# Transposes and scores share one ring of seven PSUM banks, and the exponentials run in forward order

## The chip, the cores and the metric

The kernel runs on the 8 cores of one Trainium2 chip, one batch element on each core, with no exchange between them. The metric is the device time in microseconds (us) of the slowest core. An engine name in the profile stands for: PE the matrix engine's matmuls, PEld its weight loads, DVE the vector engine, ACT the scalar engine, POOL the GpSimd engine. Each engine runs its own queue in order, and waits on semaphores that the others raise. PSUM, where PE writes its results, has 8 banks of 128 x 512 fp32.

## The reference

For each of 8 batch elements x is 2048 positions x 2048 features in fp32. There are 16 query heads of 128 features, and one key and one value head that all of them share:

```
q = (x @ q_w.T + q_b)  as 16 heads of 128;  k = x @ k_w.T + k_b;  v = x @ v_w.T + v_b
scores = q @ k.T / sqrt(128), masked causally
attn = softmax(scores);  out = (attn @ v, heads joined) @ o_w.T + o_b
x = layernorm(x + out)
x = layernorm(x + x @ (ffn_weight * scale_weight[:, None]).T + ffn_bias)
```

## The kernel before

All matmuls are in bf16. Everything is kept transposed, features on the partitions. The program is written as one list of operations in order; each engine takes its own from the list in that order, so the order of the list is the order of every queue. An operation names the events that it waits for.

*Stage A* computes k, v and the 16 heads of q into `KT`, `Vsb` and `QTO` (L259).

*Attention.* The outer loop runs over c = 0 to 3, four chunks of 512 queries. With c, the keys that count grow: 512 (c + 1). In it `step` runs over the heads, and `j` over the four blocks of 128 queries of the chunk. One head and one j are called a unit here; there are 64 units in each c. Three things are written into the list for each j, each for another head, so that they can overlap:

```
if 1 <= step <= H:          tr_unit(step - 1, c, j)
if step >= 2 and j <= c:    av_unit(step - 2, c, j)
if step < H:                sc_soft(step, c, j, sc_mms(step, c, j))
```

- `sc_mms` (L344, L353): PE computes the scores of a unit in c + 1 chunks of up to 512 keys, one bank each. The last chunk is 128 (j + 1) wide, and a second matmul adds the causal mask to it.
- `sc_soft`: DVE takes the maximum of each chunk (L372, into `mpart`), then the negative maximum over them (L376, `negm`). ACT takes the exponential of each chunk into SBUF and sums each as it goes (L393, `expS`). DVE adds the sums (L405, `den`; with one chunk that is left out) and takes the reciprocal (L410, `rcp`). ACT scales a 128 x 128 identity by it (L414, `diagP`). The exponentials go over the chunks in reversed order.
- `tr_unit` (L436): PE multiplies every 128 x 128 block of the exponentials with `diagP`, which transposes and normalizes it. Four blocks are a group and fill a bank; a unit has c + 1 groups. Each group is copied to SBUF as bf16 (`expST`), by DVE (L458) and by ACT (L462) in turn.
- `av_unit` (L480): PE multiplies four 128-key blocks of V with the transposed probabilities of a whole head, into the bank `psO`. The first of a head waits for all its transposed copies; after the last, ACT copies `psO` to SBUF (L489).

Steps 16 and 17 of each c have transposes and V matmuls alone.

*The PSUM banks.* The scores have a ring of five, the four banks of `psS` and `psU`; a chunk takes the next one, and waits until the exponential of what was in it is done. The transposes have two, `psT0` and `psT1`, in turn, given out by `use_bank`, which waits for the copy of what was in it. The eighth is `psO`.

*The last stage* does the output projection (L760), the two layer norms and the feed-forward (L826), in blocks of 512 positions. It gives `psT0`, `psT1`, `psU` and `psO` out by `use_bank`, and its matmuls wait for the end of the attention. Its weights come from HBM.

Of the kernel before, what the change touches and what calls it, by code (L numbers as in the profile page):

```python
# [16 lines left out]
S = 2048  # L17
H = 16
DK = 128
NT = 16  # L20
NCH = 4
W = 512
# [55 lines left out]
def build_program(serial=False):  # L78
# [25 lines left out]
    p = Prog(serial=serial)  # L104
# [4 lines left out]
    with st:  # L109
# [18 lines left out]
        psS = ps("psS", [128, 2048], F32)  # L128
        psT0 = ps("psT0", [128, W], F32)
        psT1 = ps("psT1", [128, W], F32)  # L130
        psO = ps("psO", [128, W], F32)
        psU = ps("psU", [128, W], F32)
# [5 lines left out]
        bank_evac = {"psT0": None, "psT1": None, "psO": None, "psU": None}  # L138
        rot_idx = [0]

        def use_bank(mm_emit, evac_emit):
            b = rot_idx[0] % len(pool_banks)
            rot_idx[0] += 1
            key, bk = pool_banks[b]
            mmw = [bank_evac[key]] if bank_evac[key] else []
            e_mm = mm_emit(bk, mmw)
            e_ev = evac_emit(bk, [e_mm])
            bank_evac[key] = e_ev
            return e_mm, e_ev

        with nc.sbuf_tensor("QTO", [128, NT * S], BF16) as QTO:
# [17 lines left out]
            with stA:  # L169
# [56 lines left out]
                for g in range(4):  # L226
# [16 lines left out]
                    _, E_vsb = use_bank(mmVT, evVT)  # L243
# [4 lines left out]
                for ot in range(NT):  # L248
# [4 lines left out]
                        waits=wq, inc="qw%d" % (ot % 2))  # L253
                    for c in range(NCH):
# [23 lines left out]
                        e_mm, e_ev = use_bank(mmQ, evQ)  # L278
# [5 lines left out]
            for q in range(4):  # L284
# [12 lines left out]
            expS8 = stB2.enter_context(  # L297
                nc.sbuf_tensor("expS8", [128, 8 * S], BF16))
            expST2 = stB2.enter_context(
                nc.sbuf_tensor("expST2", [128, 2 * NT * W], BF16))  # L300
            diagP = stB2.enter_context(
                nc.sbuf_tensor("diagP", [128, 8 * 128], BF16))
# [6 lines left out]
            E_trib = p.op("sync", lambda e: e.dma_start(  # L309
                out=trib_s[:], in_=tri_h), waits=[E_Q_all], inc="cst")  # L310

            ring_ap = [psS[:, s * W:(s + 1) * W] for s in range(4)] + [psU]
            ring_ev = [None] * 5
            ring_i = [0]

            E_comb2 = [[None] * 4, [None] * 4]
# [2 lines left out]
            E_exall2 = [[[] for _ in range(4)], [[] for _ in range(4)]]  # L319
            E_diag2v = [[None] * 4, [None] * 4]  # L320
            E_trmm2 = [[None] * 4, [None] * 4]
            E_trevV = [None, None]
            E_trevA = [None, None]
            E_trevall = [[], []]
            E_msd = [None, None]
            oev = [None]
            trctr = [0]

            def sc_mms(h, c, j):
                par = h % 2  # L330
                qt = 4 * c + j
                kext = (qt + 1) * 128
                nkc = (kext + W - 1) // W
                chunks = []
                for kc in range(nkc):
                    wdt = min(W, kext - kc * W)
                    s = ring_i[0] % 5
                    ring_i[0] += 1
                    slot = ring_ap[s]
                    w0 = [ring_ev[s], E_qevac[h][c], E_kevac[NCH - 1],  # L340
                          E_Q_all]
                    diag_chunk = (kc == nkc - 1)
                    p.op("tensor", lambda e, slot=slot, h=h, qt=qt, kc=kc,
                         wdt=wdt, dgc=diag_chunk: e.matmul(  # L344
                        slot[:, 0:wdt],
                        QTO[:, h * S + qt * 128: h * S + qt * 128 + 128],
                        KT[:, kc * W: kc * W + wdt],
                        start=True, stop=(not dgc), skip_group_check=True),
                        waits=w0,
                        inc=(None if diag_chunk else "t"))  # L350
                    if diag_chunk:
                        E_mm = p.op("tensor", lambda e, slot=slot, wdt=wdt:
                                    e.matmul(  # L353
                            slot[:, wdt - 128:wdt], ident_s[:], trib_s[:],
                            start=False, stop=True, skip_group_check=True),
                            waits=[E_trib], inc="t")
                    else:
                        E_mm = ("t", p.counts["t"])
                    chunks.append((s, slot, wdt, kc, E_mm))
                return chunks  # L360

            def sc_soft(h, c, j, chunks):
                par = h % 2
                qt = 4 * c + j
# [5 lines left out]
                for s, slot, wdt, kc, E_mm in chunks:  # L370
# [3 lines left out]
                        waits=[E_mm, E_comb2[par][j]], inc="v"))  # L374
# [4 lines left out]
                    waits=mx_all + E_exall2[par][j], inc="v")  # L379
                E_ex = None  # L380
                ex_all = []
                for s, slot, wdt, kc, E_mm in reversed(chunks):
                    if nkc == 1:
                        acc = den8[:, ncol:ncol + 1]
                        wx = [E_comb2[par][j], E_trmm2[par][j],
                              E_diag2v[par][j]]
                    else:
                        acc = dpart[:, mcol + kc:mcol + kc + 1]
                        wx = [E_comb2[par][j], E_trmm2[par][j],
                              E_dsum2[par][j]]  # L390
                    E_ex = p.op("scalar", lambda e, slot=slot, wdt=wdt,
                                kc=kc, ncol=ncol, acc=acc, par=par, qt=qt:
                                e.activation(  # L393
                        expS8[:, (par * 4 + qt % 4) * S + kc * W:
                              (par * 4 + qt % 4) * S + kc * W + wdt],
                        slot[:, 0:wdt], AF.Exp,
                        bias=negm8[:, ncol:ncol + 1], scale=1.0,
                        accum_out=acc), waits=wx, inc="a")
                    ring_ev[s] = E_ex
                    ex_all.append(E_ex)  # L400
# [19 lines left out]
            def tr_unit(h, c, j):  # L420
                par = h % 2
                qt = 4 * c + j
                base = par * NT * W
                if j == 0:
                    E_trevall[par] = []
                last_mm = None
                for g in range(c + 1):
                    cnt = min(4, qt + 1 - 4 * g)

                    def mmTR(bk, w, g=g, cnt=cnt, par=par, qt=qt, j=j):  # L430
                        w = w + [E_diag2v[par][j]] + E_exall2[par][j]
                        for i in range(cnt):
                            kt = 4 * g + i
                            ev = p.op("tensor",
                                      lambda e, bk=bk, i=i, kt=kt, par=par,
                                      qt=qt: e.matmul(  # L436
                                bk[:, i * 128:(i + 1) * 128],
                                expS8[:, (par * 4 + qt % 4) * S + kt * 128:
                                      (par * 4 + qt % 4) * S +
                                      (kt + 1) * 128],  # L440
                                diagP[:, (par * 4 + qt % 4) * 128:
                                      (par * 4 + qt % 4 + 1) * 128],
                                start=True, stop=True),
                                waits=(w if i == 0 else ()),
                                inc=("t" if i == cnt - 1 else None))
                        return ev

                    def evTR(bk, w, g=g, cnt=cnt, j=j, base=base):
                        dst = expST2[:, base:base + NT * W].rearrange(
                            "p (t w) -> p t w", t=NT)[  # L450
                            :, 4 * g:4 * g + cnt, j * 128:(j + 1) * 128]
                        srcv = bk[:, 0:cnt * 128].rearrange(
                            "p (t w) -> p t w", t=cnt)
                        eng = "vector" if trctr[0] % 2 == 0 else "scalar"
                        trctr[0] += 1
                        if eng == "vector":
                            ev = p.op("vector", lambda e, d=dst, s=srcv:
                                      e.tensor_copy(d, s), waits=w, inc="v")  # L458
                            E_trevV[par] = ev
                        else:  # L460
                            ev = p.op("scalar", lambda e, d=dst, s=srcv:
                                      e.copy(d, s), waits=w, inc="a")  # L462
                            E_trevA[par] = ev
                        E_trevall[par].append(ev)
                        return ev
                    e_mm, _ = use_bank(mmTR, evTR)
                    last_mm = e_mm
                E_trmm2[par][j] = last_mm

            def av_unit(h, c, pj):  # L470
# [22 lines left out]
            for c in range(NCH):  # L493
                for sl in range(2):
                    ev = None
# [37 lines left out]
            with stC:  # L533
# [15 lines left out]
                pool_banks[:] = [("psT0", psT0), ("psT1", psT1),  # L549
                                 ("psU", psU), ("psO", psO)]  # L550
                bank_evac["psO"] = E_attn_done

                OROT, OD = 5, 4
                FROT, FD = 3, 2
# [459 lines left out]
```

How the kernel before makes its waits and increments, by code:

```python
    def emit(self, eng_name, eng, sems):  # L62
        hi = {}
        for idx, (name, fn, waits, inc) in enumerate(self.ops):
            if name != eng_name:
                continue
            for s, v in waits:
                if hi.get(s, 0) < v:
                    eng.wait_ge(sems[s], v)
                    hi[s] = v
            ins = fn(eng)
            if inc is not None:
                if ins is None:
                    ins = eng.nop()
                ins.then_inc(sems[inc], SEMS[inc])
# [2 lines left out]
def build_program(serial=False):  # L78
# [863 lines left out]
                        pend[k]()  # L942
                    if pend_end is not None:
                        pend_end()
                    if bi + 1 < len(blocks):
                        preload(*blocks[bi + 1])
                    pend, pend_end = make_tail(kind, c)
                for k in range(len(pend)):
                    pend[k]()
                p.op("gpsimd",
                     lambda e: e.wait_ge(sems["od"], 16 * NT * NCH))
        nc._prog = p
        with nc.Block() as block:
```

## Time and profile before

| | us |
|---|---|
| median of 3 runs | 2586.69 (2586.14 to 2586.77) |
| the profiled execution, its own time | 2588.11 |
| its span on the slowest core, core 0 | 2586.6 |
| spans of the other cores | 2579.0 to 2584.9 |
| PE / DVE / ACT busy on core 0 | 1553.8 / 925.2 / 918.5 |
| mean granted clock of PE, core 0 | 0.753 |

The profile is of one execution, on its slowest core. Busy time is a mean over stages that differ: stage A ends at about 355 us, the attention runs to 1851 us, the last stage from there. A row of the timeline has the start and the duration in us, the engine, the line, the operation, what it writes and reads, how many instructions are merged in it, and in brackets for how long the engine stood before it and what it waited for. In the windows, a number behind x in parentheses counts instructions, and the clock is the share of full speed that was granted to PE.

### The profile page before, as it was taken

What the parts mean: (1) busy time and instruction counts of PE and PEld (TensorE: products, weight loads), DVE (VectorE), ACT (ScalarE), POOL (GpSimd) and SP (SyncE); (2) the same over time, 40 slices, a digit from 0 to 9 for tenths busy, and PEclk for the clock granted to TensorE, in tenths of its full rate; (3) what the DMA queues carried; (4) which work ended last, traced back from release to release, by engine and by line L of the source; (5) the groups of instructions that cost most, each with busy time, mean ns of one, the idle gap of its engine ahead of it and who ended that gap; (6) DMA issues with size and microseconds to landing.
All of it is one profiled execution on the core that took longest, in us unless ns stands there. A gap on an engine that the chain in (4) does not pass through costs nothing.

```text
span 2586.6 us, 25298 instructions; the slowest of 8 cores (2579.0 to 2586.6 us)
## 1 busy us (share of the span) xinstructions
PE 1553.8 (60%) x7077; PEld 723.6 (28%) x7216; DVE 925.2 (36%) x1985; ACT 918.5 (36%) x2270; POOL 374.6 (14%) x399
## 2 busy tenths in 40 slices
PE   0999925455544444444344445444798968968874
PEld 0444412222222222222222222222333323323321
DVE  0000024455543333433444444444216640632444
ACT  0211126555554444444444444444312321411411
POOL 0000100000000000000000000000266526535432
PEclk9999955566665666666666666666899979979976
DMA  9112698000000000000000000000255344344352
GB/s 156 24 33 41 82 111 110 1 1 1 1 1 1 1 1 0 1 1 1 1 1 1 1 1 1 1 0 1 66 171 155 107 151 149 126 163 127 101 136 98
DMA packets 43638, 137.03 MB, mean 53 GB/s; under 512 B 5835, under 2 KB 5868, under 8 KB 42988
## 3 DMA queue, kind: packets, MB, share of 16 engines
q1 hardware_dynamic: 28988, 84.02, 10.7%
q0 software_dynamic: 5296, 34.60, 9.9%
q10 hardware_dynamic: 9216, 16.78, 2.0%
q8 instruction: 61, 1.00, 0.2%
q14 instruction: 77, 0.63, 0.1%
HBM read 153.21 MB, written 33.55 MB: 72 GB/s over the span
## 4 chain that ended last, share of the span: by engine, by line
PE 43%; ACT 19%; DVE 16%; issue 12%; DMA 5%; another core or an unknown queue 2%; POOL 1%; DVEq 1%; ACTq 0%; SPq 0%; POOLq 0%
ACT expS L393 15%; PE psT L259 9%; PE psO L480 8%; DVE mpart L372 8%; PE psT L826 4%; PE psT L436 4%; PE psS L344 3%; PE psT L760 3%; DVE expST L458 3%; PE psU L826 2%; DMA wost<-wo_bf 2%; PE psU L760 2%; PE psO L826 2%; DMA trib_s<-tri 1%
## 5 line engine op out<-in xcount | busy, mean ns | idle before, releaser
L436 PE MATMUL psT<-diagP,expS 128*128 128x128 bf16 x2176 | 270.1, 284 | 687.3 <-DVE expST L458 536.8
L372 DVE TENSOR_REDUCE mpart<-psS 128x1 f32<-128x512 f32 (+3 forms) x512 | 289.9, 603 | 538.5 <-PE psS L353 366.5
L393 ACT ACTIVATE expS<-psS,negm 128x512 bf16<-128x512 f32 (+3 forms) x512 | 314.3, 620 | 448.2 <-DVE negm L376 447.2
L436 PEld LDWEIGHTS psT<-diagP,expS 128*128 128x128 bf16 x2176 | 200.4, 128 | 767.0 <-issue 762.4
L787 POOL TENSOR_TENSOR ycs<-yscr,xres 128x512 f32<-128x512 f32 x64 | 82.4, 1288 | 1674.5 <-ACT yscr L776 1562.8
L480 PE MATMUL psO<-expST,Vsb 128*128 128x512 bf16 x602 | 271.9, 599 | 48.7 <-ACT expST L462 41.7
L458 DVE CAST expST<-psT 128x512 bf16<-128x512 f32 (+1 forms) x320 | 204.1, 638 | 87.3 <-PE psT L436 86.4
L344 PE MATMUL psS<-KT,QTO 128*128 128x512 bf16 (+3 forms) x486 | 216.5, 531 | 26.6 <-ACT expS L393 22.2
L259 PE MATMUL psT<-xTbf,qwst 128*128 128x512 bf16 x1003 | 220.1, 379 | 1.3 <-ACT Vsb L241 0.2
L462 ACT CAST expST<-psT 128x512 bf16<-128x512 f32 (+3 forms) x320 | 155.8, 487 | 80.9 <-PE psT L436 80.9
L405 DVE TENSOR_REDUCE den<-dpart 128x1 f32<-128x2 f32 (+2 forms) x192 | 29.9, 156 | 414.2 <-ACT expS L393 414.2
L414 ACT ACTIVATE diagP<-ident_s,rcp 128x128 bf16<-128x128 bf16 x256 | 102.7, 401 | 144.2 <-DVE rcp L410 144.2
L760 PE MATMUL psT<-QTO,wost 128*128 128x512 bf16 x500 | 125.6, 406 | 24.2 <-DMA wost<-wo_bf 22.3
L826 PE MATMUL psT<-x1T,fwst 128*128 128x512 bf16 x500 | 123.5, 401 | 23.9 <-DMA fwst<-fw_bf 11.7
L259 PEld LDWEIGHTS psT<-xTbf,qwst 128*128 128x128 bf16 x1024 | 100.1, 98 | 121.0 <-issue 0.4
L625 DVE TENSOR_SCALAR rowb<-psS 1x512 f32<-1x512 f32 x8 | 5.4, 681 | 321.1 <-PE psS L605 321.1
L480 PEld LDWEIGHTS psO<-expST,Vsb 128*128 128x128 bf16 x640 | 81.6, 139 | 129.6 <-issue 123.6
L393 ACT ACTIVATE expS<-psU,negm 128x512 bf16<-128x512 f32 (+3 forms) x128 | 79.4, 621 | 103.7 <-DVE negm L376 103.2
L850 POOL TENSOR_TENSOR ycs<-zscr,ycs 128x512 f32<-128x512 f32 x64 | 88.6, 1384 | 170.4 <-ACT zscr L842 170.4
L273 ACT ACTIVATE QTO<-psT,qbs_s 128x512 bf16<-128x512 f32 x64 | 44.0, 687 | 177.5 <-PE psT L259 172.0
L344 PEld LDWEIGHTS psS<-KT,QTO 128*128 128x128 bf16 x512 | 71.3, 142 | 125.5 <-issue 123.0
L393 ACT ACTIVATION_READ_ACCUMULATOR expS<-psS,negm 128x1 f32 x512 | 102.1, 199 | 0.0
(76 smaller groups left out, 1727.8 us busy)
## 6 DMA issues: line engine op xcount, KB each, us to landing
wost<-wo_bf SPq DMA_DIRECT2D x64, 512.0 KB, 4.4
fwst<-fw_bf SPq DMA_DIRECT2D x64, 512.0 KB, 3.8
xres<-xT ACTq DMA_DIRECT2D x64, 256.0 KB, 4.6
outT<-ycs SPq DMA_DIRECT2D x64, 256.0 KB, 3.2
xTbf<-xT POOLq DMA_DIRECT2D x1, 8192.0 KB, 56.9
qwst<-qw POOLq DMA_DIRECT2D x16, 512.0 KB, 5.1
wo_bf<-wo POOLq DMA_DIRECT2D x4, 2048.0 KB, 77.3
fw_bf<-fw POOLq DMA_DIRECT2D x4, 2048.0 KB, 95.7
```

What stands on the lines that cost most here:

```text
L259: e.matmul(bk[:], qwst[:, (ot % 2) * D + dt * 128: (ot % 2) * D + dt * 128 + 128], xTbf[:, dt * S + c * W: dt * S + c * W + W], start=(dt ...
L344: wdt=wdt, dgc=diag_chunk: e.matmul(slot[:, 0:wdt], QTO[:, h * S + qt * 128: h * S + qt * 128 + 128], KT[:, kc * W: kc * W + wdt], start=T ...
L372: mc=mcol + kc: e.reduce_max(mpart[:, mc:mc + 1], slot[:, 0:wdt], axis=AX.X),
L393: e.activation(expS8[:, (par * 4 + qt % 4) * S + kc * W: (par * 4 + qt % 4) * S + kc * W + wdt], slot[:, 0:wdt], AF.Exp, bias=negm8[:, nco ...
L414: ncol=ncol: e.activation(diagP[:, (par * 4 + j) * 128:(par * 4 + j + 1) * 128], ident_s[:], AF.Identity, bias=0.0, scale=rcp8[:, ncol:nco ...
L436: qt=qt: e.matmul(bk[:, i * 128:(i + 1) * 128], expS8[:, (par * 4 + qt % 4) * S + kt * 128: (par * 4 + qt % 4) * S + (kt + 1) * 128], diag ...
L458: e.tensor_copy(d, s), waits=w, inc="v")
L462: e.copy(d, s), waits=w, inc="a")
L480: base=base: e.matmul(psO[:], Vsb[:, kt * 128:(kt + 1) * 128], expST2[:, base + kt * W: base + (kt + 1) * W], start=(kt == 0), stop=(kt == ...
L760: ot=ot: e.matmul(bk[:], wost[:, (ot % 2) * D + ht * 128: (ot % 2) * D + ht * 128 + 128], QTO[:, ht * S + c * W: ht * S + c * W + W], star ...
L826: ot=ot: e.matmul(bk[:], fwst[:, (ot % 2) * D + dt * 128: (ot % 2) * D + dt * 128 + 128], x1T[:, dt * W:(dt + 1) * W], start=(dt == 0), st ...
L850: pbuf=pbuf: e.tensor_tensor(pbuf[:, ot * W:(ot + 1) * W], zscr[:, (ot % 3) * W:(ot % 3) * W + W], pbuf[:, ot * W:(ot + 1) * W], AluOpType ...
```

## The change

The transposes leave `use_bank`. Scores and transposes take their banks from one ring of seven in the order in which PE does them: `psS` (four), `psU`, `psT0`, `psT1`. The wait for a slot is the copy or the exponential that read it last. The work of each operation stays. The exponentials of a unit go over its chunks in forward order. Ahead of the last stage `psT0`, `psT1` and `psU` are marked as free from the end of the attention on. The lambdas of the transposing matmuls and of the copies are the same as before, but for `skip_group_check=True`, and are left out here.

```diff
-            ring_ap = [psS[:, s * W:(s + 1) * W] for s in range(4)] + [psU]
-            ring_ev = [None] * 5
+            ring_ap = ([psS[:, s * W:(s + 1) * W] for s in range(4)]
+                       + [psU, psT0, psT1])
+            ring_ev = [None, None, None, None, None,
+                       bank_evac["psT0"], bank_evac["psT1"]]
             ring_i = [0]
...
-                    s = ring_i[0] % 5
+                    s = ring_i[0] % 7
                     ring_i[0] += 1
                     slot = ring_ap[s]
...
-                for s, slot, wdt, kc, E_mm in reversed(chunks):
+                for s, slot, wdt, kc, E_mm in chunks:
...
                 for g in range(c + 1):
                     cnt = min(4, qt + 1 - 4 * g)
-
-                    def mmTR(bk, w, g=g, cnt=cnt, par=par, qt=qt, j=j):
-                        w = w + [E_diag2v[par][j]] + E_exall2[par][j]
...
-                    e_mm, _ = use_bank(mmTR, evTR)
-                    last_mm = e_mm
+                    s = ring_i[0] % 7
+                    ring_i[0] += 1
+                    bk = ring_ap[s]
+                    w = [ring_ev[s], E_diag2v[par][j]] + E_exall2[par][j]
...
+                    E_trevall[par].append(ev)
+                    ring_ev[s] = ev
                 E_trmm2[par][j] = last_mm
...
                 bank_evac["psO"] = E_attn_done
+                bank_evac["psT0"] = E_attn_done
+                bank_evac["psT1"] = E_attn_done
+                bank_evac["psU"] = E_attn_done
```

## Rows read from the trace of the kernel before

**Rows 1.** The page, parts 1 and 2: busy; granted clock in tenths.

```profile
PE 1553.8 (60%) x7077; PEld 723.6 (28%) x7216; DVE 925.2 (36%) x1985; ACT 918.5 (36%) x2270; POOL 374.6 (14%) x399
...
PEclk9999955566665666666666666666899979979976
```

**Rows 2.** By stage: width, busy us of PE, PEld, DVE, ACT, POOL; clock, DMA.

```profile
744.00:1226.00 482.00, 219.35 (x1062) 119.57 (x1081) 190.51 (x477) 204.03 (x557) 0.00 (x0) 0.63 0.00 1
1226.00:1834.00 608.00, 287.49 (x1452) 157.89 (x1477) 258.79 (x574) 259.39 (x718) 0.00 (x0) 0.66 0.00 1
1834.00:1851.00 17.00, 13.03 (x83) 7.14 (x85) 5.00 (x8) 5.13 (x11) 0.00 (x0) 0.84 0.00 1
1851.00:2587.00 736.00, 578.61 (x2289) 218.47 (x2334) 277.86 (x320) 176.00 (x272) 352.47 (x320) 0.88 0.44 136
```

**Rows 3.** The waits, c = 3: total us, times, longest.

```profile
PE psT L436 <- DVE expST L458: 295.2, 60, 5.9
...
DVE mpart L372 <- PE psS L344: 75.9, 46, 2.0
...
DVE expST L458 <- PE psT L436: 51.7, 60, 1.2
...
DVE mpart L372 <- PE psU L344: 22.8, 12, 4.3
```

**Rows 4.** Timeline of one unit of c = 3.

```profile
1707.53 0.16 DVE L410 RECIPROCAL rcp<-den 128x1 f32<-128x1 f32 x1
1707.62 0.69 DVE L458 CAST expST<-psT 128x512 bf16<-128x512 f32 x1
...
1708.46 1.01 PE L436 MATMUL psT<-diagP,expS 128*128 128x128 bf16 x8 [4.97 <-DVE expST L458]
1709.15 0.69 DVE L458 CAST expST<-psT 128x512 bf16<-128x512 f32 x1 [0.84 <-PE psT L436]
...
1709.27 1.91 PE L480 MATMUL psO<-expST,Vsb 128*128 128x512 bf16 x4
...
1710.97 0.63 PE L344 MATMUL psS<-KT,QTO 128*128 128x512 bf16 x1
...
1711.71 0.69 DVE L372 TENSOR_REDUCE mpart<-psS 128x1 f32<-128x512 f32 x1 [1.87 <-PE psS L344]
...
1714.56 0.69 ACT L393 ACTIVATE expS<-psS,negm 128x512 bf16<-128x512 f32 x1 [2.70 <-DVE negm L376]
...
1717.70 0.16 DVE L410 RECIPROCAL rcp<-den 128x1 f32<-128x1 f32 x1
```

**Rows 5.** Timeline in one unit of c = 1.

```profile
568.69 0.69 DVE L458 CAST expST<-psT 128x512 bf16<-128x512 f32 x1
568.85 0.40 ACT L414 ACTIVATE diagP<-ident_s,rcp 128x128 bf16<-128x128 bf16 x1 [0.62 <-DVE rcp L410]
...
569.30 1.28 DVE L372 TENSOR_REDUCE mpart<-psS 128x1 f32<-128x512 f32 x2
```

**Rows 6.** The waits, c = 2.

```profile
DVE mpart L372 <- PE psS L344: 87.4, 43, 3.1
...
DVE mpart L372 <- PE psU L344: 21.0, 10, 3.2
DVE expST L458 <- PE psT L436: 19.0, 30, 0.9
...
DVE mpart L372 <- PE psT L436: 7.6, 5, 1.6
```

**Rows 7.** The waits of DVE, c = 0.

```profile
DVE mpart L372 <- PE psS L353: 11.4, 12, 1.1
```

**Rows 8.** The waits of PE, end of c = 3.

```profile
PE psT L436 <- DVE expST L458: 6.8, 4, 4.8
```

**Rows 9.** Reciprocals of c = 2, c = 3: ns, first and last start.

```profile
L410 DVE RECIPROCAL rcp<-den x64: 162/164/165, 752.5 to 1224.8; 128x1 f32<-128x1 f32 x64
...
L410 DVE RECIPROCAL rcp<-den x64: 162/164/165, 1243.4 to 1833.4; 128x1 f32<-128x1 f32 x64
```

More of the change, by code:

```diff
@@ L428, in tr_unit @@
                     cnt = min(4, qt + 1 - 4 * g)
-                    def mmTR(bk, w, g=g, cnt=cnt, par=par, qt=qt, j=j):
-                        w = w + [E_diag2v[par][j]] + E_exall2[par][j]
[L432 to L465, printed above, removed]
@@ L466, in tr_unit @@
-                    e_mm, _ = use_bank(mmTR, evTR)
-                    last_mm = e_mm
+                    s = ring_i[0] % 7
+                    ring_i[0] += 1
+                    bk = ring_ap[s]
+                    w = [ring_ev[s], E_diag2v[par][j]] + E_exall2[par][j]
+                    for i in range(cnt):
+                        kt = 4 * g + i
+                        last_mm = p.op("tensor",
+                                       lambda e, bk=bk, i=i, kt=kt, par=par,
+                                       qt=qt: e.matmul(
+                            bk[:, i * 128:(i + 1) * 128],
+                            expS8[:, (par * 4 + qt % 4) * S + kt * 128:
+                                  (par * 4 + qt % 4) * S +
+                                  (kt + 1) * 128],
+                            diagP[:, (par * 4 + qt % 4) * 128:
+                                  (par * 4 + qt % 4 + 1) * 128],
+                            start=True, stop=True, skip_group_check=True),
+                            waits=(w if i == 0 else ()),
+                            inc=("t" if i == cnt - 1 else None))
@@ new lines, in tr_unit @@
+                    dst = expST2[:, base:base + NT * W].rearrange(
+                        "p (t w) -> p t w", t=NT)[
+                        :, 4 * g:4 * g + cnt, j * 128:(j + 1) * 128]
+                    srcv = bk[:, 0:cnt * 128].rearrange(
+                        "p (t w) -> p t w", t=cnt)
+                    eng = "vector" if trctr[0] % 2 == 0 else "scalar"
+                    trctr[0] += 1
+                    if eng == "vector":
+                        ev = p.op("vector", lambda e, d=dst, s=srcv:
+                                  e.tensor_copy(d, s), waits=[last_mm],
+                                  inc="v")
+                        E_trevV[par] = ev
+                    else:
+                        ev = p.op("scalar", lambda e, d=dst, s=srcv:
+                                  e.copy(d, s), waits=[last_mm], inc="a")
+                        E_trevA[par] = ev
```

## The prediction

> **What bounds the kernel now.** I read the shares and the granted clock first [rows 1]: no engine is busy for more than 60% of the span, so either stages have different bounds or the engines wait for each other in turn. The table by stage [rows 2] settles which: in the attention for c = 2 and c = 3 (482 and 608 us) PE, DVE and ACT are each busy for 40 to 47% of the time and no DMA moves. Three engines under half busy, with nothing from outside, is a chain that passes from one to the other. The last stage (736 us, output projection and feed-forward) is PE's own.
>
> The waits of c = 3 [rows 3] show the links. PE stands for 295.2 us before transposes, released by DVE's copy at L458; DVE stands for 51.7 us before such a copy and for 75.9 + 22.8 us before its first maximum, released by PE. Each waits for the other. One unit (a head's block of 128 queries) shows the order [rows 4]: after the reciprocal DVE copies the first transposed group; only then is psT0 free, and PE writes the third and fourth group (1708.46, 8 matmuls), then the four matmuls with V (1709.27), then the scores (1710.97); the first maximum starts at 1711.71, and from there maxima, exponentials and reciprocal run without a hole until 1717.70. So a unit of 10.17 us has 4.18 us from reciprocal to first maximum, in which DVE works 1.38. In c = 1 [rows 5], where a unit has two groups for two psT banks, the copy is followed by the maximum after 0.61 us, with no wait.
>
> **The change part by part.** *The exponentials in forward order* is the same work. What moves is which ring slot is freed first. Cost 0 from reciprocal to reciprocal, for the sum waits for the last of them either way. Cover isn't needed.
>
> *The ring of 7 for scores and transposes.* Per unit PE takes c + 1 slots for transposes, then c + 1 for scores; a slot is taken again 7 takes later. Worked out for each c, with u the unit:
> - c = 3: the first three groups of u wait for copies of groups 1 to 3 of u-1, made before the maxima of u-1; group 3 for the first exponential of u-1; score chunks 0 to 2 for exponentials 1 to 3 of u-1; chunk 3 for the copy of group 0 of u.
> - c = 2: group 0 waits for an exponential of u-2, groups 1 and 2 and chunk 0 for copies of u-1, chunks 1 and 2 for exponentials 0 and 1 of u-1.
> - c = 1 and c = 0: everything is for u-1 or earlier, and no later than what PE waited for before.
>
> So the order within the queues that made PE wait for a copy which stands behind the softmax of u-1 goes away, but for one score chunk in c = 3. PE does the transposes, V and the scores of u beside the softmax of u-1, and DVE finds its input ready. What DVE loses is its idle time that PE ended.
>
> c = 3, between its first maximum and its last reciprocal [rows 3]: 75.9 + 51.7 + 22.8 = 150.4 us, less the 4.3 us before the very first maximum, which belongs to the hand-over between stages: 146.1 us. Instructions of DVE in a row also overlap: the copy lasts 0.69 us, the next starts after 0.61 [rows 5], so each wait that vanishes gives 0.08 us more. Waits: 46 + 60 + 12 - 1 = 117, so 9.4 us. Sum 155.5 us. Check on the unit of [rows 4]: 4.18 becomes 0.10 + 2 x 0.61 = 1.32, which is 2.86 us; this is a full-width unit, the mean is 155.5 / 60 = 2.6.
>
> c = 2, after its first maxima [rows 6]: 87.4 + 21.0 + 19.0 + 7.6 = 135.0 us, and 43 + 10 + 30 + 5 = 88 waits x 0.08 = 7.0. Sum 142.0 us.
>
> c = 1: the unit of [rows 5] has no such wait: 0. c = 0: DVE waits 11.4 us, 12 times about 1 us [rows 7]. That is the unit j = 0 of each head, where the matmuls with V of the head before wait for the last transposed copy, and the scores stand behind them in PE's queue. No slot has part in that, so it stays: 0.
>
> *Ends of stages* (steps 16 and 17, transposes and V with no softmax). For c = 3 this is the 17 us between 1834 and 1851 [rows 2]. PE waited 6.8 us for copies, of which 4.8 lie mostly before it [rows 8]: 2.0 inside. The four matmuls with V (1.7 us) and a group or two (0.8) can also be done before the last reciprocal. That makes some 4.5 us; the end of c = 2 alike, those of c = 1 and c = 0 less: together 10 us, an estimate between 0 and 15.
>
> *The last lines* (banks marked free by the end of attention): every matmul there waits for that event already. Cost 0. The first transposed slot changes nothing for the last stage.
>
> **Does PE fit under its cover?** Where a stall goes, PE is next. At the slow clock a 512-column matmul starts every 0.43 us (four in 1.70 [rows 4], so 1.2 GHz), a transposing one every 0.10. A head of c = 3 has 58 transposes, 16 matmuls with V, and scores worth 14.5 full matmuls and 4 for the mask: 5.9 + 6.9 + 6.2 + 0.4 = 19.4 us. From the first to the last reciprocal of c = 3 there are 63 units in 590.0 us [rows 9]; less 155.5 it is 434.5, or 6.9 a unit and 27.6 a head. PE would be at 70% of it. The tightest place is in c = 3: group 3 of u starts when the first exponential is done and its sum read out, about 0.8 us after its start (0.69 for the exponential [rows 4], the rest an estimate); then 0.4 + 1.7, and 0.74 from the start of chunk 0 to the maximum [rows 4]: 3.7 us. DVE wants it after 3.14 (first exponential to reciprocal, 1714.56 to 1717.70) + 1.32 = 4.46 us, in narrower units from 4.1. Margin 0.4 to 0.7 us at the slow clock. Chunk 3 waits for the first copy: ready at about 0.8 + 0.1 + 1.0 = 1.9 us after the reciprocal, wanted at 1.32 + 3 x 0.6 = 3.1. ACT has diagP, two copies and at times psO between reciprocal and exponential: it starts 0.3 after the reciprocal and takes 0.4 [rows 5]; with DVE's 0.69 for each copy that is 2.8 us, against 1.3 + 2.8 for DVE's copies and maxima. All hidden; if the cover of the first went by x us, it would cost x in each of 60 units.
>
> The rows show a mean granted clock of 0.63 and 0.66 in these stages, and 0.88 in the last one, where PE seldom stands [rows 2]; the V matmuls at 1.2 GHz come after 4.97 us in which PE stood [rows 4]. The Trainium skill's page "TensorE: Matmul & The Clock Gate", sections "What's actually happening" and "A second HAM failure mode: psum-queue depth-cycling", says that the array gets the full rate only when it has been busy, and that a kernel which cycles PSUM banks with short idle times flips between both. By the first PE would speed up when its work is packed; by the second it would stay slow often. It decides between the margins above and larger ones, and bears on how likely the first rival is; the sum is the same.
>
> **The sum.** 155.5 + 142.0 + 10 = 307 us. Profiled execution: 2588.1 us (span 2586.6 and 1.5 around it). 2588.1 - 307 = 2281; it stands 1.4 above the median of the runs (2586.7), so 2280 us.
>
> **Rivals.**
> - *PE becomes the bound.* Now PE has one continuous queue through both stages, and if it stays slow, or starts late through waits on ACT's copies, scores come after DVE wants them. For it: margins under 1 us, clock levels that change. Against: 70% at the slow clock. If it comes later by 0.5 us than it may, 60 + 60 units cost 60 us: 2340. Range 2310 to 2400.
> - *The wait only moves.* In c = 3 eight takes a unit run over seven slots, so chunk 3 is tied to a copy behind the softmax. If the whole score set, not only chunk 3, hung on it, nothing would be gained there: 155 back, 2435; if in both stages, 2587. Against: chunk 3 is the last in the queue, and 1.2 us early by the working above.
> - *Slower: the clock of the last stage.* A denser attention could be followed by a lower granted clock in the 736 us where PE is the bound [rows 2]. At 0.88 it takes 736; if all of it goes with the clock, it would eat 307 us when it took 1043, which is a granted clock of 0.88 x 736 / 1043 = 0.62. At 0.55 it gives 2280 + 442 = 2720. For it: 0.6 levels exist in this trace. Against: they stand where PE is idle for half of the time, and the last stage starts the same way.
>
> **How the numbers follow.** Forecast 0.81; PE the bound 0.12; the wait only moves 0.04 (half of it without any gain); slower 0.03. The likeliest gives 2280. Its low end: ends of stages 15 instead of 10, and the 11 us of c = 0 gone with a faster clock: 2264. Its high end: no gain at the ends (10) and no overlap (16): 2306. To hold 8 in 10, the upper end goes into the PE case: 2262 to 2325. Changes under 0.2% (5 us) can't be told from none here. Faster 0.95: all of the forecast, of PE, and half of the third; same 0.02; slower 0.03.
>
> **What would show it.** In the changed profile: DVE's idle time before L372 and before the copy, ended by PE, near zero in c = 2 and c = 3; reciprocal to first maximum 1.3 us in c = 3 (4.2 now) and 0.7 to 1.2 in c = 2; reciprocals of c = 3 within about 434 us (590 now), of c = 2 within 330 (472 now [rows 9]); c = 1 unchanged, and c = 0 with its 1 us waits; the last stage still 736 us; granted clock in the attention not lower. PE's waits should name exponentials (L393), not copies. Wrong if the maxima still wait for scores, which would be PE late, or if copies, maxima or exponentials grow longer with PE working beside them; in c = 1 they do not.

## The result and the profile after

The changed kernel takes 2277.45 us (median of 10 runs) against 2588.1 us in the runs beside it: the ratio is 0.879, with a 95% interval of 0.8757 to 0.8824. The forecast was 2280 us. Some executions of every kernel here, whatever the kernel, take a few per cent longer on some of the cores (two of these ten, 2325 and 2331 us), and the ratios leave them out. The profiled execution took 2279.16 us, with a span of 2277.6 us on its slowest core, core 7.

The windows of the changed kernel, with the columns of [rows 2]: c = 2, c = 3 (here from about the first to the last reciprocal), last stage.

```profile
749.80:1086.80 337.00, 211.26 (x1099) 91.89 (x1097) 181.45 (x476) 198.78 (x555) 0.00 (x0) 0.71 0.00 1
1099.30:1532.50 433.20, 266.99 (x1425) 129.90 (x1425) 242.07 (x562) 245.50 (x701) 0.00 (x0) 0.70 0.00 1
...
1544.80:2277.60 732.80, 578.02 (x2336) 217.33 (x2334) 280.35 (x320) 176.00 (x272) 355.30 (x320) 0.89 0.45 137
```

The reciprocals, first and last start, c = 2 and c = 3, to set beside [rows 9]:

```profile
L412 DVE RECIPROCAL rcp<-den x64: 164/164/165, 757.8 to 1086.7; 128x1 f32<-128x1 f32 x64
...
L412 DVE RECIPROCAL rcp<-den x64: 164/164/167, 1099.4 to 1532.4; 128x1 f32<-128x1 f32 x64
```

From first to last reciprocal it is 328.9 us in c = 2 (472.3 before) and 433.0 us in c = 3 (590.0). The last stage is as long as it was, 732.8 against 736. The windows of [rows 2] take in the hand-over between stages; from first to last reciprocal PE is busy for 206 us in c = 2 and 267 in c = 3, where it was 215 and 277, but in 0.70 and 0.73 of the time. Its mean granted clock is 0.71 in c = 2 and 0.70 in c = 3, where it was 0.63 and 0.66.

One unit of c = 3 in the timeline, to set beside [rows 4]:

```profile
1490.38 0.16 DVE L412 RECIPROCAL rcp<-den 128x1 f32<-128x1 f32 x1
1490.48 0.69 DVE L458 CAST expST<-psT 128x512 bf16<-128x512 f32 x1
...
1491.09 0.68 DVE L458 CAST expST<-psS 128x512 bf16<-128x512 f32 x1
...
1491.68 1.28 DVE L374 TENSOR_REDUCE mpart<-psS 128x1 f32<-128x512 f32 x2
...
1494.38 0.69 ACT L395 ACTIVATE expS<-psS,negm 128x512 bf16<-128x512 f32 x1 [2.50 <-DVE negm L378]
...
1495.31 0.58 PE L439 MATMUL psS<-diagP,expS 128*128 128x128 bf16 x4 [2.60 <-ACT expS L395]
...
1497.39 0.63 PE L346 MATMUL psS<-KT,QTO 128*128 128x512 bf16 x1
...
1497.42 0.16 DVE L412 RECIPROCAL rcp<-den 128x1 f32<-128x1 f32 x1
...
1498.73 0.68 DVE L374 TENSOR_REDUCE mpart<-psS 128x1 f32<-128x512 f32 x1
```

After the reciprocal (1490.38) the two copies and the first maximum follow each other with 0.6 us between the starts: 1.30 us to the maximum, where it was 4.18. Over the units of a stage the median of this stretch went from 3.98 to 1.30 us in c = 3 and from 3.44 to 0.81 in c = 2. From the reciprocal to the last maximum no row of DVE has a bracket any more, it finds its input ready. The one wait that DVE has left in a unit is for ACT's last exponential, before it adds the sums. In the whole of c = 3 this is its only wait:

```profile
DVE den L407 <- ACT expS L395: 177.8, 63, 3.0
```

Before the change it stood for the same 177.8 us in 63 waits there, and 146.1 us more for PE. The rows of PE show why: the fourth group of the next unit starts at 1495.31, when the first exponential of this unit is out, and its first score, after V, at 1497.39. That is 3.01 us after the first exponential, and the maximum that wants it starts at 1498.73.

The waits of c = 3, all engines, with the columns of [rows 3]:

```profile
PE psS L439 <- ACT expS L395: 81.0, 34, 3.5
...
PE psT L439 <- ACT expS L395: 43.2, 18, 2.9
...
PE psU L439 <- ACT expS L395: 21.0, 9, 2.7
...
PE psS L346 <- DVE expST L458: 7.5, 14, 0.8
```

PE's 295 us before transposes, which DVE's copy had ended, are gone. What it waits for is the first exponential (81.0 + 43.2 + 21.0 us), time in which nobody waits for PE. The score chunk tied to a copy is the row of 7.5 us and two smaller ones of the same kind, into psT (2.6 us) and psU (0.8): 10.9 us in 20 waits. DVE has no wait for PE left in this stretch.

In c = 2 PE still waits for copies before transposes, 51.6 us in all, besides 68 us for exponentials. Such waits are what the count of slots in the prediction names (groups 1 and 2 wait for copies of u-1), and they too cost nothing: DVE has no wait for PE's scores there, and 0.3 us before one copy. In c = 0 DVE's waits are what they were [rows 7], now spread over the ring's banks:

```profile
DVE mpart L374 <- PE psS L355: 6.7, 7, 1.1
DVE mpart L374 <- PE psT L355: 3.7, 4, 1.0
DVE mpart L374 <- PE psU L355: 2.0, 2, 1.0
```

### The profile page after: what moved, and what is told of

It is laid out like the page before. It is cut to its first block, busy times and chain, and to the rows that moved or that the text cites. A ratio compares the mean times of both kernels' runs of the same rounds, so it can differ in the third digit from the quotient of the medians.

```text
span 2277.6 us, 26021 instructions; the slowest of 8 cores (2265.3 to 2277.6 us)
## 1 busy us (share of the span) xinstructions
PE 1537.1 (67%) x7216; PEld 670.5 (29%) x7216; DVE 907.8 (40%) x1985; ACT 905.9 (40%) x2270; POOL 377.4 (17%) x399
## 3 DMA queue, kind: packets, MB, share of 16 engines
q1 hardware_dynamic: 28988, 84.02, 12.2%
## 4 chain that ended last, share of the span: by engine, by line
PE 45%; DVE 16%; ACT 14%; issue 14%; DMA 6%; another core or an unknown queue 3%; POOL 1%; DVEq 1%; ACTq 0%; SPq 0%; POOLq 0%
ACT expS L395 11%; PE psT L259 10%; DVE mpart L374 8%; PE psO L479 7%; PE psT L828 4%; PE psT L762 3%; PE psS L346 3%; PE psU L828 3%; DMA wost<-wo_bf 3%; PE psO L828 2%; PE psU L762 2%; DVE ycs L721 2%; PE psS L439 2%; DMA trib_s<-tri 2%
## 5 line engine op out<-in xcount | busy, mean ns | idle before, releaser
L374 DVE TENSOR_REDUCE mpart<-psS 128x1 f32<-128x512 f32 (+3 forms) x367 | 206.4, 600 | 374.5 <-PE psS L355 370.2
L395 ACT ACTIVATE expS<-psS,negm 128x512 bf16<-128x512 f32 (+3 forms) x367 | 224.5, 618 | 224.7 <-DVE negm L378 224.0
L439 PE MATMUL psS<-diagP,expS 128*128 128x128 bf16 x1250 | 149.6, 263 | 149.2 <-ACT expS L395 112.2
L346 PE MATMUL psS<-KT,QTO 128*128 128x512 bf16 (+3 forms) x367 | 159.6, 484 | 64.7 <-ACT expS L395 41.0
L439 PEld LDWEIGHTS psS<-diagP,expS 128*128 128x128 bf16 x1250 | 104.3, 118 | 195.7 <-issue 191.8
L395 ACT ACTIVATE expS<-psT,negm 128x512 bf16<-128x512 f32 (+3 forms) x185 | 114.5, 623 | 104.7 <-DVE negm L378 104.1
L439 PE MATMUL psT<-diagP,expS 128*128 128x128 bf16 x605 | 75.4, 261 | 78.3 <-ACT expS L395 62.5
L458 DVE CAST expST<-psS 128x512 bf16<-128x512 f32 (+2 forms) x183 | 114.3, 637 | 2.7 <-PE psS L439 2.7
L374 DVE TENSOR_REDUCE mpart<-psT 128x1 f32<-128x512 f32 (+3 forms) x185 | 107.5, 607 | 10.0 <-PE psT L346 6.3
L346 PE MATMUL psT<-KT,QTO 128*128 128x512 bf16 (+3 forms) x185 | 84.9, 489 | 36.0 <-ACT expS L395 26.3
```

The costliest lines, as they stand in the source:

```text
L346: wdt=wdt, dgc=diag_chunk: e.matmul(slot[:, 0:wdt], QTO[:, h * S + qt * 128: h * S + qt * 128 + 128], KT[:, kc * W: kc * W + wdt], start=T ...
L374: mc=mcol + kc: e.reduce_max(mpart[:, mc:mc + 1], slot[:, 0:wdt], axis=AX.X),
L395: e.activation(expS8[:, (par * 4 + qt % 4) * S + kc * W: (par * 4 + qt % 4) * S + kc * W + wdt], slot[:, 0:wdt], AF.Exp, bias=negm8[:, nco ...
L439: qt=qt: e.matmul(bk[:, i * 128:(i + 1) * 128], expS8[:, (par * 4 + qt % 4) * S + kt * 128: (par * 4 + qt % 4) * S + (kt + 1) * 128], diag ...
L458: e.tensor_copy(d, s), waits=[last_mm],
```

## The experiments

All of them are the changed kernel or the kernel before with one edit, the last with two. In each profile the stretch from first to last reciprocal of a stage was read; it differs by about 1 us between cores unless said, which makes it a finer measure than the total: the first reciprocal of c = 0 came between 357 and 396 us in cores of these runs, in a part of the program that is the same in all.

**The order of the exponentials alone undone**

```diff
-                for s, slot, wdt, kc, E_mm in chunks:
+                for s, slot, wdt, kc, E_mm in reversed(chunks):
```

> The shared ring of 7, but the exponentials in reversed order as before. By the theory (PE runs ahead because of which slots come free early): in c = 3 the fourth transposed group now waits for the last exponential instead of the first. From there 0.1 to 0.4 us of transposes, 1.7 of V matmuls and 0.74 to the first maximum are 2.6 to 2.9 us, and DVE wants the scores 1.85 us after the last exponential, so 0.7 to 1.0 us late in each of 60 units: about 48 us more than the changed kernel, 2325 us (2310 to 2345), all of it in c = 3. In c = 2 only chunk 1 waits for the last exponential, wanted 1.9 us later: nothing lost. Rival: the order is only a detail and the ring alone carries the gain: 2277 us, c = 3 unchanged at 433 us.

Measured: ratio to before 0.8992 (0.897 to 0.9013), which is 2327 us (0.8992 x 2588); the profiled execution took 2330 us. c = 2 stays at 329 us, c = 3 takes 482.4 us on this core and up to 488.7 on others, 49 to 56 more than with the order changed. The reciprocals of c = 3 and one unit in the timeline:

```profile
L412 DVE RECIPROCAL rcp<-den x64: 163/164/165, 1098.0 to 1580.4; 128x1 f32<-128x1 f32 x64
```

```profile
1555.06 0.69 ACT L395 ACTIVATE expS<-psU,negm 128x512 bf16<-128x512 f32 x1
...
1555.98 0.37 PE L439 MATMUL psU<-diagP,expS 128*128 128x128 bf16 x2 [2.81 <-ACT expS L395]
...
1557.85 1.06 PE L346 MATMUL psT<-KT,QTO 128*128 128x512 bf16 x2
...
1558.60 1.29 DVE L374 TENSOR_REDUCE mpart<-psT 128x1 f32<-128x512 f32 x2 [1.01 <-PE psT L346]
```

PE does what the expectation says: it stands 2.81 us until the last exponential is out, then come two transposes, V, the scores, and the maximum at 1558.60 had to wait 1.01 us. Over c = 3 DVE waited 44.0 us for PE's scores, 52 times; with 0.08 us of lost overlap each that is 48 us, of the 49.4 that this core lost. The ring without the order is worth 261 us (2588 - 2327), the order with the ring about 50.

**The order alone done, with the old banks**

```diff
-                for s, slot, wdt, kc, E_mm in reversed(chunks):
+                for s, slot, wdt, kc, E_mm in chunks:
```

> The kernel before (5 score slots, 2 transpose banks in turn), with the exponentials in forward order. By the theory nothing is gained, because the third transposed group still waits for a copy behind the softmax: within 0.2% of before, about 2588 us, reciprocal to first maximum still 3.9 to 4.2 us in c = 3. Rival: the order of the exponentials frees the scores earlier and is worth part of the gain: 20 us or more less than before.

Measured: ratio 0.998 (0.9957 to 1.0003), no difference. c = 3:

```profile
L410 DVE RECIPROCAL rcp<-den x64: 161/164/165, 1267.8 to 1858.1; 128x1 f32<-128x1 f32 x64
```

It takes 590.3 us, as before. So the order is worth 50 us with the ring and nothing without it.

**Seven banks, but not shared** (the first line changed is that of the scores, the second that of the transposes)

```diff
+            ring_t = [0]
...
-                    s = ring_i[0] % 7
+                    s = ring_i[0] % 4
...
-                    s = ring_i[0] % 7
-                    ring_i[0] += 1
+                    s = 4 + ring_t[0] % 3
+                    ring_t[0] += 1
```

> Seven banks as in the changed kernel, forward exponentials, but two rings: 4 slots for scores, 3 for transposes. By the theory c = 2 keeps its whole gain (329 us from first to last reciprocal), since its three groups fit; in c = 3 the fourth group waits for the copy of the first of the same unit, behind the softmax: reciprocal to first maximum 0.1 + 0.69 + 0.14 + 0.27 + 1.7 + 0.74 = 3.6 us instead of 1.3, 56 units x 2.3 us and a little for step 1: 130 to 140 us more than the changed kernel, about 2412 us. Rival: a third transpose bank is what was missing and sharing is no matter: 2277 to 2290 us.

Measured: 2421.85 us, ratio 0.9369 (0.9335 to 0.9404). The reciprocals of c = 2 and c = 3, and three of the waits of c = 3:

```profile
L413 DVE RECIPROCAL rcp<-den x64: 162/164/165, 757.0 to 1086.1; 128x1 f32<-128x1 f32 x64
...
L413 DVE RECIPROCAL rcp<-den x64: 162/164/165, 1102.3 to 1667.9; 128x1 f32<-128x1 f32 x64
```

```profile
PE psT L440 <- DVE expST L459: 181.6, 40, 5.6
...
DVE mpart L375 <- PE psS L347: 126.6, 60, 2.4
...
PE psU L440 <- DVE expST L459: 90.1, 20, 5.4
```

c = 2 keeps all (329.1 us), c = 3 takes 565.6 us, 132.6 more than with the shared ring (564.9 to 565.6 on the eight cores). Once a unit, 40 + 20 times, PE waits for DVE's copy again, and DVE for PE's scores (126.6 us in 60 waits, with the overlap 131). The third bank is enough where a unit has three groups; where it has four it brings 24 us of 157. A split that gives the scores fewer than four slots wasn't run: in c = 3 the fourth chunk would have to wait for an exponential of its own unit, and that one for the maximum over all four.

**A ring of six**

```diff
-                    s = ring_i[0] % 7
+                    s = ring_i[0] % 6
```

> The changed kernel with a shared ring of 6 (one psT bank left out). By the theory c = 0 to 2 lose nothing; in c = 3 the fourth group waits for the second exponential instead of the first, which brings the first score to 4.1 to 4.4 us after the first exponential, wanted at 4.1 to 4.45: at most 0.1 us late in three of four units, 5 us in all: 2275 to 2290 us. Rival: the gain grows with the number of slots, 5+2 to 7 shared, and a slot is worth a good part of it: 2330 us or more.

Measured: 2285.16 us, ratio 0.881 (0.8791 to 0.8829); c = 3:

```profile
L412 DVE RECIPROCAL rcp<-den x64: 162/164/165, 1100.3 to 1534.7; 128x1 f32<-128x1 f32 x64
```

434.4 us, 1.4 more than with seven (up to 435.3 on other cores); the intervals of the two totals overlap. The seventh bank is worth next to nothing; what counts is that the banks are shared.

**More work for PE**

```diff
+                    for _ in range(2 * j if c == 3 and kc == 0 else 0):
+                        p.op("tensor", lambda e, ...: e.matmul(
+                            slot[:, 0:wdt], QTO[...], KT[...],
+                            start=True, stop=True, skip_group_check=True),
+                            waits=w0)
```

> The changed kernel with superfluous work for PE: in c = 3 the matmul of score chunk 0 is done 2j more times (0, 2, 4, 6 for j = 0 to 3), each overwritten by the next, the output is the same. By the theory PE has a margin in which work is free: in the changed trace the first score matmul starts about 2.8 us after the first exponential, is usable after 0.74, and is wanted at 4.1 to 4.45, so the margin is 0.9 us for j = 0 and about 0.5 for j = 1 to 3. At 0.43 us each (slow clock) the units come 0, 0.4, 1.2 and 2.1 us later: 59 us in all, 2336 us; if the clock rises to 0.22 us each, 0, 0, 0.4, 0.8: 19 us, 2296. Rival: PE is already the bound of the changed kernel, so every superfluous matmul costs its full 0.22 to 0.43 us, for j = 1 as well: c = 3 longer by 192 x 0.22 to 0.43 = 42 to 83 us, with 0.43 to 0.86 us in j = 1.

Measured: 2286.3 us, ratio 0.8829 (0.8782 to 0.8875). The reciprocals of c = 3, DVE's waits for PE there, and the windows of c = 2 and c = 3:

```profile
L420 DVE RECIPROCAL rcp<-den x64: 162/164/165, 1092.0 to 1540.2; 128x1 f32<-128x1 f32 x64
```

```profile
DVE mpart L382 <- PE psS L354: 7.3, 11, 1.9
DVE mpart L382 <- PE psT L354: 2.8, 7, 1.0
DVE mpart L382 <- PE psU L354: 2.5, 5, 0.8
```

```profile
750.00:1079.00 329.00, 201.83 (x1047) 88.63 (x1067) 178.19 (x470) 195.49 (x545) 0.00 (x0) 0.71 0.00 1
1092.00:1540.00 448.00, 281.91 (x1582) 139.27 (x1611) 244.09 (x561) 245.82 (x701) 0.00 (x0) 0.79 0.00 1
```

192 matmuls more cost 15.2 us (448.2 against 433.0; 445.3 on the core with the least), or 0.06 to 0.08 us each. DVE waited for PE 23 times, 12.6 us in all, at most 1.9 us, which with 0.08 us of overlap each is 14.4 of the 15.2; 48 of the 64 units have added work. So most of it was free, and PE was not the bound. The size was nearer to the fast clock's 19 us than to the slow clock's 59, and the windows show it: 0.79 granted in c = 3, where the changed kernel has 0.70, and c = 2 without added work keeps 0.71. PE's own busy time in c = 3 rose by no more than some 18 us (265.4 us in core 4 of the changed kernel, 282.9 in core 7 here, where few records are missing), while 192 matmuls take 82 us at 0.43 us each: the rest was made up by the other matmuls, which ran at the fast clock more often. So two things made the added work cheap, the time in which DVE did not yet want the scores, and the clock; this run does not part them.

**V behind the softmax**

```diff
-                        if step >= 2 and j <= c:
-                            av_unit(step - 2, c, j)
                         if step < H:
                             sc_soft(step, c, j, sc_mms(step, c, j))
+                        if step >= 2 and j <= c:
+                            av_unit(step - 2, c, j)
```

> The changed kernel with the V matmuls (and the copy of their sum) put behind the scores and the softmax of the unit in the list, instead of between transposes and scores. By the theory for c = 0 (the 1 us waits there have nothing to do with slots, but with the V matmuls ahead of the scores in PE's queue) reciprocal to first maximum of j = 0 falls from 1.37 to 0.39 us, 16 times: c = 0 shorter by 15 us, 120 instead of 135.4, the rest the same or a little longer at the ends of stages: 2258 to 2270 us. Rival: the wait stems from the ring or from the clock and stays: c = 0 at 135 us, 2277.

Measured: 2271.17 us, ratio 0.8769 (0.8738 to 0.88); the intervals of this and of the changed kernel overlap, so the total does not settle it. The stages in the trace do. c = 0, and the timeline of units j = 0 and j = 1 of one head:

```profile
L412 DVE RECIPROCAL rcp<-den x64: 162/164/165, 363.0 to 488.6; 128x1 f32<-128x1 f32 x64
```

```profile
424.25 0.16 DVE L412 RECIPROCAL rcp<-den 128x1 f32<-128x1 f32 x1 [1.03 <-ACT expS L395]
...
424.55 0.28 DVE L374 TENSOR_REDUCE mpart<-psT 128x1 f32<-128x128 f32 x1
...
426.37 0.57 ACT L488 CAST QTO<-psO 128x512 bf16<-128x512 f32 x1
...
426.48 0.15 DVE L378 TENSOR_REDUCE negm<-mpart 128x1 f32<-128x1 f32 x1
...
427.10 0.49 ACT L395 ACTIVATE expS<-psS,negm 128x256 bf16<-128x256 f32 x1
```

c = 0 takes 125.6 us instead of 135.4, on all eight cores within 0.1. The first maximum of j = 0 comes 0.30 us after the reciprocal and without a wait, where it had waited about 1 us [rows 7]; so the wait did stem from V ahead of the scores. Of 15 us expected 10 were found: ACT's copy of `psO` (426.37, 0.57) now stands ahead of the exponential of j = 1, which starts 0.62 us after its negative maximum; 0.3 is usual. DVE's waits for ACT before the reciprocals of c = 0 are 61.0 us, where they were 56.4, and that is the missing 5. At the end of c = 3 the stage takes 14.6 us, 2.4 more.

**DVE's copies behind the maxima**

The chain that is left is reciprocal, copies, maxima, exponentials. This edit defers DVE's copies in the list: ACT copies the even groups ahead of the exponentials as before, DVE the odd ones (in c = 0 the only one) after the negative maximum. It is more than a delay: in c = 2, where the two engines had taken the three groups of a unit in turn, ACT now has two of them each time, and in c = 0 DVE has all; what this share is worth was not run alone. `copyV` issues the copy and notes it as the event that frees the slot.

```diff
+            def run_late():
+                for f in late:
+                    f()
+                late.clear()
...
                     waits=mx_all + E_exall2[par][j], inc="v")
+                run_late()
                 E_ex = None
...
-                    eng = "vector" if trctr[0] % 2 == 0 else "scalar"
+                    if g % 2 == 1 or c == 0:
+                        late.append(copyV)
+                        continue
```

> The changed kernel with DVE's part of the copies moved behind the negative maximum of the unit in DVE's queue (ACT copies groups 0 and 2, DVE groups 1 and 3; in c = 0 DVE copies all). By the theory DVE and ACT in turn are the bound now (reciprocal, copies, maxima, exponentials), so copies that DVE does while ACT has the exponentials come off the chain: 0.6 us a unit in c = 1, 0.6 to 1.1 in c = 2, 1.2 in c = 3, together up to 37 + 50 + 73 = 160 us. But transposes of the next unit start later, and PE does V before the scores: in c = 3 the first score is usable 4.5 us after the first exponential at the slow clock and wanted after 3.0, so the gain of c = 3 is lost there and only c = 1 and c = 2 keep most of it: 2190 us (2150 to 2240). Rival: PE or the copies themselves bound the kernel, nothing is gained: 2277 or more.

Measured: ratio 0.8543 (0.8498 to 0.8587), 2212 us; the profiled execution took 2211.6. Reciprocals of c = 1, 2, 3 and DVE's waits in c = 3:

```profile
L418 DVE RECIPROCAL rcp<-den x64: 163/164/165, 502.6 to 721.9; 128x1 f32<-128x1 f32 x64
...
L418 DVE RECIPROCAL rcp<-den x64: 162/164/165, 733.7 to 1031.4; 128x1 f32<-128x1 f32 x64
...
L418 DVE RECIPROCAL rcp<-den x64: 162/164/165, 1045.7 to 1466.9; 128x1 f32<-128x1 f32 x64
```

```profile
DVE mpart L379 <- PE psS L346: 30.1, 25, 1.6
DVE mpart L379 <- PE psT L346: 16.7, 14, 1.6
DVE mpart L379 <- PE psU L346: 9.2, 7, 1.6
```

Shorter by 19, 31 (29 to 34 by core) and 12 us. Up to 37 and 50 were expected of c = 1 and c = 2, and nothing or little of c = 3; the total is 22 us above the 2190. The copies are off the chain, but in c = 3 DVE waits 56 us for scores: now the transposes start later and V is ahead of the scores. That such waits would come in c = 3 alone was wrong: DVE also waits for scores in c = 1 (15.7 us, 15 times) and in c = 2 (13.6 us, 22 times). The next run shows that the order in PE's queue is what is short, not PE.

**Both**

> Both edits together: DVE's copies behind the negative maximum, V matmuls behind the softmax. By the theory the scores are then ready in c = 3 at 2.9 to 3.7 us after the first exponential, wanted at 3.0, and c = 0 loses its 1 us waits: 2277 - 37 - 50 - 60 - 15 = 2115 us (2095 to 2170), the first maximum 0.1 to 0.8 us after the reciprocal in all stages. Rival: with a period of 5.7 us and 4.9 us of matmuls at the slow clock PE becomes the bound: more than 2170.

Measured: ratio to before 0.8178 (0.8143 to 0.8212), about 2116 us (0.8178 x 2588). The profiled execution took 2148.3 us: on its slowest core the attention starts late (first reciprocal at 395.5 us, 357.8 on the core with the earliest); c = 3 takes 366.6 to 367.4 us on all eight. Reciprocals of c = 0 to 3, the largest of DVE's waits for PE in c = 3 (there are three more, 1.3 us together), and the window of c = 3:

```profile
L418 DVE RECIPROCAL rcp<-den x64: 162/164/165, 395.5 to 515.7; 128x1 f32<-128x1 f32 x64
...
L418 DVE RECIPROCAL rcp<-den x64: 163/164/165, 523.5 to 725.6; 128x1 f32<-128x1 f32 x64
...
L418 DVE RECIPROCAL rcp<-den x64: 162/164/165, 737.4 to 1020.1; 128x1 f32<-128x1 f32 x64
...
L418 DVE RECIPROCAL rcp<-den x64: 162/164/165, 1035.1 to 1402.2; 128x1 f32<-128x1 f32 x64
```

```profile
DVE mpart L379 <- PE psS L355: 1.8, 8, 0.5
```

```profile
1035.00:1402.00 367.00, 217.36 (x1390) 110.11 (x1414) 231.51 (x561) 254.86 (x700) 0.00 (x0) 0.86 0.00 1
```

120.2, 202.1, 282.7 and 367.1 us, against 135.4, 238.7, 328.9 and 433.0: 164 us less than the changed kernel, where 162 were worked out beforehand from DVE's instructions. In c = 1 and c = 2 DVE's waits for PE are down to 0.3 us each. PE at a clock of 0.86 is no bound. This version beats both kernels.

## Why the prediction was right, by its steps

| term | forecast us | measured us, span of core 0 before to core 7 after |
|---|---|---|
| c = 3, DVE's idle time ended by PE | 155.5 | 157.0 (590.0 to 433.0) |
| c = 2, the same | 142.0 | 143.4 (472.3 to 328.9) |
| c = 0 and c = 1 | 0 | 0 (135.3 and 238.7, each within 0.2) |
| ends of stages | 10 | 14 |
| last stage | 0 | 3 |
| before the attention | 0 | -8 |

The two large terms came within 1.6 us. They are a count, idle time of one engine with one releaser, plus 0.08 us of overlap for each wait, and [rows 3, 5, 6] gave all of it. The idle time came out within 0.2 us: from first to last reciprocal DVE stands 146.1 us less in c = 3 and 135.2 less in c = 2. What is left, 10.9 and 8.2 us, is overlap, forecast at 9.4 and 7.0.

*The ring.* Which event each slot waits for, worked out by counting slots, fits every stage: the waits of PE name the events that it gives in c = 2 and c = 3, and c = 0 and c = 1 kept their time. One sign that the prediction asked for did not follow from its own count: PE's waits should name exponentials, not copies, and in c = 2 they name both. The kernels with the order undone, with split rings and with six banks put a late event ahead of PE in c = 3 alone, and moved c = 3 alone, by +49 to 56, +133 and +1.4 to 2.3 us where +48, +130 to 140 and +5 followed from the same count. This also settles the second rival: the tied score chunk costs PE 10.9 us and DVE nothing.

*The order of the exponentials.* "The same work", cost 0, holds: alone, with the old banks, the order changes nothing that can be measured. That it frees the first slot early was used for the margin of PE, but its worth was not stated in the prediction; it is 50 us of the 310.

*The margin of PE.* Forecast at 0.4 to 0.7 us at the slow clock. In the unit above it is 0.6: the first score starts at 1497.39, is usable 0.74 later [rows 4], and is taken at 1498.73. The added matmuls show that there is such a margin: with none added DVE has no wait, with 192 added 12.6 us. The first rival, PE the bound, falls. It was given 0.12; nothing in the changed kernel came near to it.

*Ends of stages.* The term that was mis-sized, 14 for 10. From the last reciprocal of one stage to the first of the next (for c = 3 to the first matmul of the last stage) it was 8.7, 12.4, 18.5, 17.3 us, and is 8.0, 9.9, 12.7, 12.2. Each of these differs by up to 2.5 us between the cores of one execution, so the 14 are good to a few us. At the end of c = 3 PE's waits for copies [rows 8] are gone; for a bank it waits once, for `psO`:

```profile
PE psO L479 <- ACT QTO L488: 0.8, 1, 0.8
```

*Last stage.* Its clock is 0.89 against 0.88; the third rival (a clock lower by a third) falls. The 3 us are less than the cores of one execution differ there (726 to 736 us before). The 8 us before the attention lie in a part that the change does not touch, and no run shows what they come from; in the runs of the kernels above that part is between 357 and 396 us long on single cores. Without it and the 3 us of the last stage the sum would be 314 instead of 309. The terms of the change thus gave 7 us more than the 307 that were forecast, and the late start took them back: that the total came within 2 us is in part luck.

## What to carry to other kernels

When two engines stand for each other in turn, count per unit which slot is taken again after how many takes, and name the event that frees it: a wait for something that is queued behind the next softmax makes the engines take turns, and a bank more does little where the event stays the same (in c = 3 six shared banks 434 us, seven split ones 566, and 590 before). The saving can be read off beforehand as the idle time of the engine that remains the bound, ended by the engine that is freed, as long as that engine then fits under its cover; the same sum, read backwards, gave what the kernels with the order undone (48 of 49 us), with split rings (131 of 133) and with added matmuls (14.4 of 15.2) lost. Then ask what is left on the chain and could be queued behind it: the copies moved behind the maxima, with V behind the scores, gave another 164 us.

## What the runs showed of the hardware

PE's granted clock in c = 3 was 0.66 before, 0.70 after, 0.79 with 192 superfluous matmuls, and 0.86 in the last version: in these three more work per us went with a higher clock. It does not follow the work per us alone. With V behind the softmax c = 3 has the same matmuls in the same time, and the clock is 0.65, on the other cores up to 0.68, where all cores of the changed kernel have 0.70 to 0.72:

```profile
1086.30:1519.50 433.20, 298.92 (x1415) 139.38 (x1414) 241.89 (x562) 245.35 (x700) 0.00 (x0) 0.65 0.00 1
```

Why is open. But it shows that the clock does not carry the gain: at 0.65, as low as before the change, c = 3 takes 433 us, because PE is not the bound.

Added work cost 0.06 to 0.08 us a matmul, at most a fifth of the 0.43 us that one takes at the slow clock [rows 4].

The clock went back and forth between its two levels before and after: in c = 3 the trace has 103 to 110 changes of level, by core, before and 76 to 94 after, in a stage a quarter shorter. Per us that is about as often, so seven shared banks instead of five and two did not make it worse, and the mean clock rose. The Trainium skill, "TensorE: Matmul & The Clock Gate", section "A second HAM failure mode: psum-queue depth-cycling", tells of a kernel whose clock goes back and forth in this way, since PE stands briefly between groups of matmuls while it cycles through PSUM banks. The trace agrees that the clock changes often here; that the cycling itself is the cause, it does not show.
